# Moving the weight-quantising work of an attention loop to the head ends, dropping two waits, and keeping one head on chip

## The reference

```
x = x + layernorm(attn(layernorm(x)))          # 16 heads of 128, causal, S = D = 2048
x = x + layernorm(ffn(layernorm(x)))           # I = 4096

attn:  Q = (X Wq' + bq) * s ; K = (X Wk' + bk) * s ; V = X Wv' + bv
       out = softmax(causal(Q K')) V  per head ;  out Wo' + bo
ffn:   h = relu(bitlinear(x, w_up))^2 ;  bitlinear(h, w_down)
bitlinear(x, w): x rounded to 8 bits per row, w replaced by
       clip(round(w / mean|w|), -1, 1) * mean|w|         # three values
```

## Time and profile before

| | us |
|---|---|
| median of 3 runs | 5664.41 (5659.16 to 5669.59) |
| the profiled execution | 5661.84 |
| its span on core 7, first to last instruction | 5660.2 |
| spans of the 8 cores | 5584.0 to 5660.2 |
| PE busy / DVE busy / ACT busy / POOL busy | 2892.4 / 1890.4 / 824.1 / 380.3 |
| mean granted TensorE clock, core 7 | 0.789 of full |

### The profile page before, as it was taken

How to read it: one execution, slowest core, us unless ns; L and a number is a source line. 1 busy time by engine, 2 the same in 40 slices (tenths; PEclk the granted TensorE clock), 3 DMA queues, 4 the chain that set the end, 5 groups by cost and what they waited for, 6 DMA issues and landing times.

```text
span 5660.2 us, 34301 instructions; the slowest of 8 cores (5584.0 to 5660.2 us)
## 1 busy us (share of the span) xinstructions
PE 2892.4 (51%) x10388; PEld 1096.3 (19%) x10388; DVE 1890.4 (33%) x2752; ACT 824.1 (15%) x929; POOL 380.3 (7%) x716
## 2 busy tenths in 40 slices
PE   0000174554845557455566454378475476377366
PEld 0000031111311113111122111023132132133122
DVE  1136212222132221322213222234563562662662
ACT  1100000222002221022220222100112111210220
POOL 0001110000110001100010000100000000000000
PEclk9999986777956778677787777578687788698688
DMA  6677631111121111211111111221334444444443
GB/s 97 94 189 253 153 52 35 49 42 46 23 60 37 47 49 31 63 38 38 40 49 34 49 41 65 102 104 52 115 112 104 130 116 112 124 114 116 137 112 112
DMA packets 358600, 472.12 MB, mean 83 GB/s; under 512 B 161553, under 2 KB 317201, under 8 KB 337681
## 3 DMA queue, kind: packets, MB, share of 16 engines
q0 software_dynamic: 69136, 251.74, 16.0%
q1 hardware_dynamic: 289282, 218.19, 14.3%
HBM read 385.92 MB, written 83.89 MB: 83 GB/s over the span
## 4 chain that ended last, share of the span: by engine, by line
PE 41%; DVE 16%; DMA 14%; ACT 13%; issue 6%; DVEq 4%; SPq 3%; POOL 2%; ACTq 0%; POOLq 0%
PE psB L1045 7%; ACT pt L645 6%; PE psB L435 4%; PE psB L473 4%; PE psB L1171 4%; PE psB L559 4%; DMA xt<-x 3%; PE psB L789 3%; PE psB L666 3%; DMA qfm_ar<-qtile 3%; PE psB L505 2%; PE psA L632 2%; PE psA L636 2%; PE psB L677 2%; PE psB L672 2%
## 5 line engine op out<-in xcount | busy, mean ns | idle before, releaser
L1045 PE MATMUL psB<-wsl_f,qfm_ar 128*128 128x512 bf16 x2048 | 479.5, 399 | 354.5 <-DMA qfm_ar<-qtile 354.5
L1171 PE MATMUL psB<-wsl_f,qfm_ar 128*128 128x512 bf16 x2048 | 500.7, 410 | 267.6 <-DMA qfm_ar<-qtile 220.7
L645 ACT ACTIVATE pt<-psA,negC 128x1024 bf16<-128x1024 f32 x320 | 356.5, 1114 | 711.6 <-PE psA L636 709.4
L666 PE MATMUL psB<-pt,ones_bf 128*128 128x512 bf16 x320 | 150.5, 470 | 586.4 <-DVEq L91 325.5
L559 PE MATMUL psB<-y_fm,wsl 128*128 128x512 bf16 x1024 | 283.3, 439 | 134.2 <-DVEq L91 134.2
L1045 PEld LDWEIGHTS psB<-wsl_f,qfm_ar 128*128 128x128 bf16 x2048 | 207.6, 102 | 626.3 <-issue 408.7
L296 PE MATMUL psB<-smallA,ones_f 128*1 128x4 f32 x2 | 0.2, 166 | 625.4 <-DVEq L91 625.4
L1171 PEld LDWEIGHTS psB<-wsl_f,qfm_ar 128*128 128x128 bf16 x2048 | 211.1, 104 | 557.2 <-issue 353.4
L655 DVE TENSOR_TENSOR pt<-pt,strip 128x512 bf16<-128x512 bf16 x256 | 97.4, 422 | 625.4 <-ACT pt L645 625.4
L789 PE MATMUL psB<-wo_bf,y_fm 128*128 128x512 bf16 x1024 | 271.6, 433 | 61.8 <-DVEq L91 55.0
L435 PE MATMUL psB<-y_fm,wsl 128*128 128x512 bf16 x1024 | 229.6, 388 | 98.8 <-DMA wsl<-wkt 55.4
(11 more groups left out here) (159 smaller groups left out, 3333.1 us busy)
## 6 DMA issues: line engine op xcount, KB each, us to landing
wsl_f<-tup_sp SPq DMA_DIRECT2D x512, 128.0 KB, 2.7
wsl_f<-tdn_sp SPq DMA_DIRECT2D x512, 128.0 KB, 2.7
wch<-wupt POOLq DMA_DIRECT2D x16, 2048.0 KB, 9.0
wch<-wdnt POOLq DMA_DIRECT2D x32, 1024.0 KB, 5.6
wqch<-wupt POOLq DMA_DIRECT2D x32, 1024.0 KB, 5.6
wqch<-wdnt POOLq DMA_DIRECT2D x32, 1024.0 KB, 5.4
xt<-x SPq DMA_DIRECT2D x16, 1024.0 KB, 12.3
tup_sp<-tq_bf POOLq DMA_DIRECT2D x128, 128.0 KB, 2.1
```

What stands on the lines that cost most here:

```text
L645: exp_done[(hq, u)] = p.op("scalar", lambda e, sb=sb: e.activation(out=p_t[sb][:], in_=S2[sb][:, 0:1024], func=ACT.Exp, bias=negC[:], scal ...
L666: p.op("tensor", lambda e, sb=sb, u=u: e.matmul(PS[5][:, :], ones_bf[:, :], p_t[sb][:, 0:512], start=(u == 0), stop=False))
L1045: t_mm = p.op("tensor", lambda e, par=par, c=c, t=t, j=j: e.matmul(PS[par][:, :], q1fm[:, c * 512 + t * 128: c * 512 + (t + 1) * 128], wsl ...
L1171: t_mm = p.op("tensor", lambda e, par=par, c=c, t=t, s=s: e.matmul(PS[par][:, :], q2fm[:, c * 512 + t * 128: c * 512 + (t + 1) * 128], wsl ...
```

## The change

Three edits.

- The two waits of TensorE on `p.n(SV)` and `p.n(SA)` ahead of a group's first Q projection are deleted. The wait for `lq` stays.
- The weight units inside a head move. Instead of one behind each of the blocks qb = 1, 2 and 3, three in a row are emitted behind the last block. Their number is the same: 3 + 4 x 3 in a group, and four behind the last head.
- The last head (h = 15) writes its result with the same VectorE multiplication straight into its slot of `y1_fm`. Its four stores to `o_sp` and its reload are gone. The other heads keep the old lines, in the `else:` branch.

```diff
@@ ahead of the Q projections of a group @@
-        p.wait("tensor", SV, p.n(SV))
-        p.wait("tensor", SA, p.n(SA))
         p.wait("tensor", lq)
         for hl in range(4):
@@ end of a block @@
-                p.op("vector", lambda e, qpar=qpar: e.tensor_tensor(
-                    out=ot_b[qpar][:], in0=PS[6 + qpar][:, :], in1=rcp_t[qpar][:],
-                    op=ALU.mult))
-                o_evac.append(p.sig("vector", SV))
-                p.wait("gpsimd", SV, o_evac[hq])
-                o_spw.append(p.dma("gpsimd", lambda e, h=h, qb=qb, qpar=qpar: e.dma_start(
-                    out=o_sp[h, :, qb * 512:(qb + 1) * 512], in_=ot_b[qpar][:]),
-                    f"osp{hq % 2}"))
+                if h == H - 1:
+                    p.op("vector", lambda e, qpar=qpar, h=h, qb=qb: e.tensor_tensor(
+                        out=y1_fm[:, h * S + qb * 512: h * S + (qb + 1) * 512],
+                        in0=PS[6 + qpar][:, :], in1=rcp_t[qpar][:], op=ALU.mult))
+                    o_evac.append(p.sig("vector", SV))
+                    o_spw.append(o_spw[-1])
+                else:
...
                 hq += 1
-                if qb >= 1:
-                    wq_emit_load(1)
-                    wq_emit_quant(1)
+            for _ in range(3):
+                wq_emit_load(1)
+                wq_emit_quant(1)
         q_proj_last[grp] = last_qproj[0]
@@ reload @@
-    for hh in range(H):
+    for hh in range(H - 1):
 ...
+    o_rld.append(o_rld[-1])
```

More of the change, by code:

```diff
@@ L698, in build_core @@
                     p.wait("vector", o_spw[hq - 2])
-                p.op("vector", lambda e, qpar=qpar: e.tensor_tensor(
-                    out=ot_b[qpar][:], in0=PS[6 + qpar][:, :], in1=rcp_t[qpar][:],
-                    op=ALU.mult))
-                o_evac.append(p.sig("vector", SV))
-                p.wait("gpsimd", SV, o_evac[hq])
-                o_spw.append(p.dma("gpsimd", lambda e, h=h, qb=qb, qpar=qpar: e.dma_start(
-                    out=o_sp[h, :, qb * 512:(qb + 1) * 512], in_=ot_b[qpar][:]),
-                    f"osp{hq % 2}"))
+                if h == H - 1:
[5 more added lines that the diff above has]
+                else:
+                    p.op("vector", lambda e, qpar=qpar: e.tensor_tensor(
+                        out=ot_b[qpar][:], in0=PS[6 + qpar][:, :], in1=rcp_t[qpar][:],
+                        op=ALU.mult))
+                    o_evac.append(p.sig("vector", SV))
+                    p.wait("gpsimd", SV, o_evac[hq])
+                    o_spw.append(p.dma("gpsimd", lambda e, h=h, qb=qb, qpar=qpar: e.dma_start(
+                        out=o_sp[h, :, qb * 512:(qb + 1) * 512], in_=ot_b[qpar][:]),
+                        f"osp{hq % 2}"))
                 hq += 1
-                if qb >= 1:
-                    wq_emit_load(1)
-                    wq_emit_quant(1)
+            for _ in range(3):
+                wq_emit_load(1)
+                wq_emit_quant(1)
         q_proj_last[grp] = last_qproj[0]
```

## The result

The changed kernel takes 6058.11 us (median of 8 runs, 6044.94 to 6081.38) against 5664.66 us for the kernel before (8 runs). The ratio is 1.0706, with a 95% interval of 1.0686 to 1.0726: slower by 393 us. The prediction was 6062 us, slower, in a range of 6020 to 6105. In a few executions of some kernels the cores of one die run at a lower granted clock and the time is about 1% longer; the ratios leave these out and the medians hold them, which shifts no difference between medians by more than 5 us.

A forecast was written before the change was run, and what follows sets the result against it. No engine was busy much over half the span, so waits were taken to bound the kernel. Moved units +428.8 us, dropped waits -22, last head -6.5: 400.3 us slower, 6062 us forecast, range 6020 to 6105.

The forecast's parts named there:

- Mid-head units cost nothing, head-end units a whole pitch: VectorE, attention heads: two units per head leave free places for head ends, each adding 13.4 us between units; 428.8 us.
- TensorE can run ahead by part 0 alone: Next head's Q projection: only its first part runs beside the units, so both extra pitches are bare, 26.8 us per head.
- The dropped waits give 22 us: Group starts: part 0 of the Q projection runs beside the units, saving 5.5 us per group, 22 us in all.
- The last head gives 6.5 us: Behind head 15: GpSimd no longer waits for its blocks, so the next unit's load is issued early, saving 6.5 us.
- The clock's mean stays: TensorE in the attention: heads average 84.7 us and no net change is taken, nor any slower restart after longer stalls.
- The forecast's own sign of being wrong: Attention of a head: a length other than 82 to 91 us would show the prediction wrong.
- The sum: Whole kernel: 428.8 us for moved units, less 22 for dropped waits and 6.5 for the last head, 400.3 us slower.
- The moved units hide: Rival, next head's Q projection: the three units are covered there, leaving only the gains, 5633 us; 2%.
- Only VectorE's work is bare: Rival, head ends: loads run ahead, so a unit costs 4.85 us instead of 13.4, giving 5788 us; 4%.
- The dropped waits do nothing: Rival, group starts: L585 waits as long as L559 did, giving 6084 us, inside the range; 6%.
- The clock turns: Rival, attention: longer stalls shift TensorE's clock, all heads long 6155 us, all short 6012; 7% above 6105, 5% below 6020.
- The formula of the Trainium skill: Weight unit loads: 2.0 us plus bytes over 436,000 per us, 4.4 us for 1 MB, making the moved units cost 390 us.

The follow-up runs named there:

- experiments 6 and 7: Kernel before, no unit at a head end: units behind qb = 0, 1, 2 (5529.63 us); or all three edits' waits and write, loads ahead, 64 units inside heads (5257.08 us).
- experiment 5: The changed kernel with one more load call ahead of the very first unit, so loads run one unit ahead: 5784.31 us, ratio 1.0203 to the kernel before.
- experiment 3: The kernel before with only TensorE's two waits ahead of a group's first Q projection deleted: 5640.89 us, ratio 0.9953.
- experiment 1: The kernel before with only the units behind qb = 1, 2, 3 moved behind the last block: 6102.75 us, ratio 1.0767.
- experiment 2: The kernel before with one unit per head moved instead of two, so two stand behind qb = 3: 5889.20 us, ratio 1.0389.
- experiment 6: The kernel before with units behind qb = 0, 1, 2 instead of 1, 2, 3, none at a head end: 5529.63 us, ratio 0.9745.
- experiment 7: The kernel before without the two waits, with direct write, loads one unit ahead and all 64 units inside the heads: 5257.08 us, ratio 0.9265.

## Why the prediction was right, point by point

- **Mid-head units cost nothing, head-end units a whole pitch.** Right, and the step on which all hangs. The move alone gave 436 us where the sum had 428.8, and one moved unit gave 222 where half the sum is 214. The pitch in the changed kernel is 13.5 us in the mean over the 16 head ends, with 13.4 taken; the last head's second pitch alone was 16.0. A head end inside a group grew by 26.8 us in the mean, as forecast.
- **TensorE can run ahead by part 0 alone.** Right: 39.65 us of standing still, 39 forecast; ahead of the K projection up to 41.5 us, 41 forecast.
- **The dropped waits give 22 us.** The mechanism was right; the single edit measured 26 us, at the upper bound given, and its trace 6.5 us per group where 5.5 was taken. The 1 us was a mis-sized term: the sum charged it for an L585 at the low clock and a slower part 1. But part 1 was slow before too, and from the first L585 to `negC` group 0 took 24.2 us before and 23.5 in the changed kernel. The wait left over is 30 to 32 us, not 28: part 0, now right behind the squaring loop, took 4.23 us in the changed kernel instead of 6.40, and the stall behind it, whose end VectorE sets, is longer by as much.
- **The last head gives 6.5 us.** Seen in the trace as forecast (0.31 instead of 6.46 us); in the times 9 us, with no change not excluded.
- **The clock's mean stays.** Right for this change: 84.6 against 84.7 us per head. The forecast's own sign of being wrong, a head outside 82 to 91 us, did come: the shortest took 80.4 us. The sign was drawn too tight, for head 14 had taken 81.5 before the change, and the mean, which is what the sum uses, did not move. That the stall's length adds nothing to the restart is shown by the stretch from the first L585 (L583) of a head to its `negC`: it was 25.3 us before and 25.3 in the changed kernel, in the mean over the twelve heads that don't start a group. The restart does have a price, some 3 us per head end, as experiments 6 and 7 showed by removing the stall; it was there before and after alike, and so not in the difference.
- **The sum.** The three edits alone give 436 - 26 - 9 = 401 us, the whole change 393, the sum 400.3. So no sign is seen that the edits touch each other, though the interval of the first alone reaches from 411 to 458 us. That the forecast of the time came within 4 us is in part luck: the ratio's interval leaves 389 to 411 us for the change.
- **The rivals.** "The moved units hide" fell with the 39.65 us. "Only VectorE's work is bare" fell with the 13.4 us; experiment 5 shows what it would have needed, and that a single `tq_bf` would still have kept it at 9.4. "The dropped waits do nothing" fell with experiment 3. "The clock turns" did not come about.
- **The formula of the Trainium skill**, "DMA: Bandwidth & Descriptors", section "Anatomy of one DMA — SWDGE (gpsimd) path", with 4.4 us per 1 MB load, stayed below the rows here too: the loads' median from issue to landing was 5.7 us in the changed kernel. The 390 us that it would give for the moved units lie outside the interval of experiment 1.

## What to carry to other kernels

Side work on an in-order engine costs nothing where what follows it there isn't needed for a while, and its whole length where what follows starts the next phase. Here, moving 32 free units to a bare place cost 436 us, and putting all 64 under cover gave 411. Before moving such a unit, look in the brackets of the next instruction behind it: a releaser from another engine means cover; "issue" means that it comes late, by a few us (experiment 6) or by the unit's whole pitch (experiment 1). And look at the order of load and store in the queue: one load issued ahead changed the pitch from 13.4 to 9.4 us.

## What the hardware showed that was not expected

The slow restart behind a stall of TensorE does not cost more for a longer stall. Standing still for 12.44 and for 39.65 us was followed both times by an L585 (L583) of 2.04 and 2.05 us and a part 1 of 5.2 us. Over the twelve heads that don't start a group, the stretch from the first L585 to `negC` takes these times:

| mean stall | from L585 to `negC`, mean | kernel |
|---|---|---|
| 12.3 us | 25.3 us | before |
| 24.6 us | 23.9 us | experiment 5 |
| 25.8 us | 24.9 us | experiment 2 |
| 39.3 us | 25.3 us | changed |
| 2.0 us | 22.5 us | experiment 6 |
| 2.0 us | 22.2 us | experiment 7 |

So a restart cost 1.5 to 3 us. Why it was cheaper in experiment 5 is open; its length of stall doesn't explain it, since experiment 2 had nearly the same.

In the profiled execution of all nine kernels, cores 1, 3, 5 and 7 had the longer spans (in the changed kernel 6045 to 6058 us against 5958 to 5999). The difference arises before the attention: group 0's K projection begins at 675 to 687 us on these cores and at 621 to 638 on the others. In the kernel before, the 48 loads of `w_up` and `w_down` for the sums of the first stage take 7.0 to 7.2 us in the median to land on them and 5.9 to 6.3 on the others; what makes it slower was not looked for.
